# Second layer's experts: every quarter of the weights split into high and low halves, in five places, two low halves made by POOL

## What is computed

```python
router_probs = softmax(x @ gate_w + gate_b)
expert_values, expert_indices = top_k(router_probs, 2)
expert_values = expert_values / (sum(expert_values) + 1e-09)
h = gelu(x @ ew1[e] + eb1[e])            # 8 experts, 512 -> 2048
y = h @ ew2[e] + eb2[e]                  # 2048 -> 512
moe_out = sum over the two chosen experts of expert_values * y
```

## Time and profile before

| | |
|---|---|
| median of 3 runs | 2242.58 us (2241.16 to 2250.36) |
| profiled execution, its own time | 2245.86 us |
| its span, first to last instruction | 2244.1 us |
| PE busy | 2113.2 us (94%) |
| DVE busy | 1282.6 us (57%) |
| ACT busy | 1027.1 us (46%) |
| POOL busy | 519.6 us (23%) |
| the stage of the change | 1848.6 us to the end |

### The profile page before, as it was taken

The page is one execution under the profiler, slowest core; times in us unless marked ns, Lnnn a source line. Parts: engine busy times, 40 slices in busy tenths (PEclk is TensorE's granted clock), DMA queues, the critical chain, the costliest instruction groups (busy, mean ns, idle before and its releaser), DMA issues. The chain is left out here.

```text
span 2244.1 us, 39533 instructions
## 1 busy us (share of the span) xinstructions
PE 2113.2 (94%) x13342; PEld 1495.8 (67%) x13343; DVE 1282.6 (57%) x2751; ACT 1027.1 (46%) x2379; POOL 519.6 (23%) x503
## 2 busy tenths in 40 slices
PE   6999999997999999999888999999989889999998
PEld 4777777775954444444466777777769337777775
DVE  4677777776772222222347777777650127777776
ACT  2566666665321111111215666666653015666655
POOL 4000000001463554555420000000013002223331
PEclk9999999997999999999999999999989999999999
DMA  5011100012143999999821000000121426656661
GB/s 184 28 33 34 33 29 19 24 60 79 38 192 118 341 305 330 335 348 265 233 81 54 28 28 28 28 28 1 77 102 56 124 90 233 253 207 220 228 223 19
DMA packets 63756, 288.19 MB, mean 128 GB/s; under 512 B 10626, under 2 KB 10796, under 8 KB 44292
## 3 DMA queue, kind: packets, MB, share of 16 engines
q1 hardware_dynamic: 43892, 247.41, 29.9%
q0 software_dynamic: 19728, 38.97, 8.0%
HBM read 259.82 MB, written 32.93 MB: 130 GB/s over the span
## 5 line engine op out<-in xcount | busy, mean ns | idle before, releaser
L795 ACT ACTIVATE probs<-ps,less_max 100x360 f32<-100x360 f32 (+1 forms) x384 | 212.0, 561 | 166.9 <-DVE less_max L625 88.0
L1707 PE MATMUL pgu<-ring,xT 128*128 x560 | 266.0, 598 | 3.9 <-DVE xT L1787 2.0
L781 ACT ACTIVATE pTs<-pt 128x300 f32<-128x300 f32 x512 | 189.5, 425 | 125.6 <-PE pt L504 124.5
L1707 PEld LDWEIGHTS pgu<-ring,xT 128*128 128x128 f32 x560 | 100.2, 191 | 109.1 <-issue 108.7
L504 PE MATMUL pt<-ident,probs 100*128 100x100 f32 (+1 forms) x1152 | 137.6, 257 | 30.2 <-ACT pTs L781 26.7
L2094 DVE TENSOR_TENSOR ws_low<-first,ws_high 128x2048 fp32r<-128x2048 f32 x63 | 143.0, 2291 | 24.1 <-ACT ws_high L2025 24.1
L504 PEld LDWEIGHTS pt<-ident,probs 100*128 100x128 f32 (+1 forms) x1152 | 116.4, 141 | 60.4 <-issue 36.5
L381 PE MATMUL po<-first 128*128 128x512 f32 (+1 forms) x564 | 143.9, 404 | 1.4 <-DVEq L683 1.4
L381 PE MATMUL pp<-first 128*128 128x512 f32 x564 | 143.0, 402 | 1.2 <-DVE first L405 1.2
L625 DVE CUSTOM_DVE_ANT_0 ps<-ps,madd 100x362 f32<-100x362 f32 (+1 forms) x256 | 128.8, 565 | 22.9 <-PE ps L490 22.7
L377 PE MATMUL po<-first 128*128 128x362 f32 (+1 forms) x720 | 136.6, 339 | 2.8 <-DVE first L414 1.4
(11 more groups left out here) (330 smaller groups left out, 4208.9 us busy)
## 6 DMA issues: line engine op xcount, KB each, us to landing
ring<-in_l_ew SPq DMA_DIRECT2D x64, 1536.0 KB
first<-in_l_ew SPq DMA_DIRECT2D x32, 1024.0 KB, 8.5
w<-in_l_ew SPq DMA_DIRECT2D x32, 1024.0 KB, 8.7
xnT<-in_ctxT SPq DMA_DIRECT2D x14, 1444.0 KB, 6.8
first<-in_l_up SPq DMA_DIRECT2D x2, 4096.0 KB, 13.8
b<-in_l_eb SPq DMA_DIRECT2D x8, 1024.0 KB, 4.6
wd<-in_l_down SPq DMA_DIRECT2D x2, 2048.0 KB, 7.8
xn_rows<-mid SPq DMA_DIRECT2D x16, 200.0 KB
```

Source lines behind the costliest of these rows:

```text
L781: act.activation(pTs[:, g % 2, j, 3 * half:3 * half + 3, :].rearrange("k c q -> k (c q)"), pt[:, half, 0:3 * S], ACT.Copy).then_inc(t_out, 1)
L795: act.activation(probs[g % 2 * HPC + j][:, k0:k1], ps[j][0:S, 0:k1 - k0], ACT.Exp, bias=less_max[:, g, seg, j:j + 1], scale=-1.0 if masked ...
L1707: last = pe.matmul(pgu[p][:, :], xT[p][:, c, :], wgu[c], start=c == 0, stop=c == DC - 1)
```

## The change

All eight quarters are split now. The places are five: up quarters 0 to 3 in places 0, 1, 2, 3 and down quarters 0 to 3 in 0, 1, 2, 4. The two new places and `hb` lie at addresses that earlier stages use for other tiles (hence ACT's wait for `sum_begun`). The low halves of up quarter 3 and of down quarter 3 are made by POOL (`last_lows`), in its loop behind the gather and the scatter; DVE makes the other six. The plain FP32 products, `hT` and their semaphores go; PE no longer reads the tile's expert. On PE `down(0)` comes ahead of `turned(1)`. On ACT and DVE the order of the turns is new: DVE makes the low halves of the next tile's up quarters 0 and 1 ahead of yb and y, and that of quarter 2 behind them. The diff, cut to its core:

```diff
@@ -1841,20 +1841,22 @@
         xT = [sb(f"xT{part}", [P, DC, P], F32R) for part in ("_high", "_low")]
 
 
-        WS, WS_DOWN = (0, 1, 2, 1), {1: 0, 2: 2}
+
+
+        WS, WS_DOWN = (0, 1, 2, 3), (0, 1, 2, 4)
         ws = [[sb(f"ws{n}{part}", [P, 4, 512], F32R) for part in ("_high", "_low")] for n in range(2)]
...
         ws.append([sb(f"ws2{part}", [P, 4, 512], F32R) for part in ("_high", "_low")])
+        ws += env.more_ws
         x_high = sem("x_high")
         w_high, w_low = [sem(f"w_high{q}") for q in range(NQ)], [sem(f"w_low{q}") for q in range(NQ)]
-        hb = [sb(f"hb{n}", [P, 512]) for n in range(2)]
+        hb = env.hb
         h = [sb(f"h{n}", [P, 512]) for n in range(2)]
-        hT = sb("hT", [P, 2, FQ, P])
-        hs = [sb(f"hs{part}", [P, 2, FQ, P], F32R) for part in ("_high", "_low")]
+        hs = [sb(f"hs{part}", [P, NQ, FQ, P], F32R) for part in ("_high", "_low")]
         yb = sb("yb", [P, D])
-        d_high, d_low = ({q: sem(f"{name}{q}") for q in WS_DOWN} for name in ("d_high", "d_low"))
+        d_high, d_low = ([sem(f"{name}{q}") for q in range(NQ)] for name in ("d_high", "d_low"))
         hs_high, hs_ready = sem("hs_high"), sem("hs_ready")
         px = pb("px", [P, DC, P])
         pu = [pb(f"pu{n}", [P, 512]) for n in range(2)]
...
@@ -1894,10 +1896,8 @@
 
                         if q < NQ:
                             used, value = w_low[q], e and ended + 1
-                        elif q - NQ in WS_DOWN:
+                        else:
                             used, value = d_low[q - NQ], e and ended + 1
-                        else:
-                            used, value = down_mm, e and ended * NQ + (q - NQ + 1)
                         if q == NQ:
                             load(b1[:, :], b_up[e:e + 1, :].broadcast_to([P, I1]), b1_in, biased, e and ended * NQ + 1)
                         if e > 0 or q >= NQ:
@@ -1936,16 +1936,31 @@
                     pool.wait_ge(x_mm, t)
                     pool.sem_inc(passed, 1)
                     fetch(t)
+                def last_lows(t):
+
+                    pool.wait_ge(w_high[3], t + 1)
+                    pool.sem_inc(passed, 1)
+                    pool.tensor_tensor(ws[WS[3]][1][:, :, :], w[3][:, :, :], ws[WS[3]][0][:, :, :].bitcast(F32),
+                                       ALU.subtract).then_inc(w_low[3], 1)
+                    pool.wait_ge(d_high[3], t + 1)
+                    pool.sem_inc(passed, 1)
+                    pool.tensor_tensor(ws[WS_DOWN[3]][1][:, :, :], w[NQ + 3][:, :, :],
+                                       ws[WS_DOWN[3]][0][:, :, :].bitcast(F32), ALU.subtract).then_inc(d_low[3], 1)
 
                 pool.sem_inc(index_ready, 1)
+                pool.sem_inc(w_low[3], 1)
+                pool.sem_inc(d_low[3], 1)
                 fetch_next(1)
+                last_lows(0)
                 pool.wait_ge(env.sum_begun, 16 * G)
                 pool.sem_inc(passed, 1)
                 fetch_next(2)
                 add_rows(0, True)
+                last_lows(1)
                 with pool.Fori(3, n_tiles + 1) as t:
                     fetch_next(t)
                     add_rows(t - 2)
+                    last_lows(t - 1)
...
@@ -1963,8 +1978,6 @@
 
                 rows_turned(0)
                 with pe.Fori(0, n_tiles) as t:
-                    e = expert_of(pe, t)
-
                     def up(q):
                         pe.wait_ge(w_low[q], t + 2)
                         if q >= 2:
@@ -1979,7 +1992,7 @@
                     def turned(q):
                         pe.wait_ge(h_ready, t * NQ + q + 1)
                         if q >= 2:
-                            pe.wait_ge((hT_ready, hs_ready)[q % 2], t * 2 + 1)
+                            pe.wait_ge(hs_ready, t * NQ + q - 1)
                         for f in range(FQ):
                             last = pe.transpose(ph[q % 2][:, f, :], h[q % 2][:, f * P:(f + 1) * P], ident[:, :])
                         last.then_inc(h_mm, 1)
@@ -1987,14 +2000,9 @@
                     def down(q):
                         if q == 0:
                             pe.wait_ge(y_ready, t + 1)
-                        if q in WS_DOWN:
-                            pe.wait_ge(d_low[q], t + 2)
-                            pe.wait_ge(hs_ready, t * 2 + q // 2 + 1)
-                            parts = [(hs[i][:, q // 2], ws[WS_DOWN[q]][j]) for i, j in PARTS]
-                        else:
-                            pe.wait_ge(w_in[NQ + q], e * 16 + 16)
-                            pe.wait_ge(hT_ready, t * 2 + q // 2 + 1)
-                            parts = [(hT[:, q // 2], w[NQ + q])]
+                        pe.wait_ge(d_low[q], t + 2)
+                        pe.wait_ge(hs_ready, t * NQ + q + 1)
+                        parts = [(hs[i][:, q], ws[WS_DOWN[q]][j]) for i, j in PARTS]
                         for f in range(FQ):
                             for n, (hidden, weight) in enumerate(parts):
                                 last = pe.matmul(pd[:, :], hidden[:, f, :], weight[:, f, :], start=q + f + n == 0,
@@ -2005,8 +2013,8 @@
                     up(1)
                     turned(0)
                     up(2)
+                    down(0)
                     turned(1)
-                    down(0)
                     up(3)
                     turned(2)
                     down(1)
@@ -2054,27 +2062,31 @@
                     def hidden_out(q):
 
                         act.wait_ge(h_mm, t * NQ + q + 1)
-                        dst, ready = (hs[0], hs_high) if q in WS_DOWN else (hT, hT_ready)
-                        act.activation(dst[:, q // 2], ph[q % 2][:, :, :], ACT.Copy).then_inc(ready, 1)
+                        act.activation(hs[0][:, q], ph[q % 2][:, :, :], ACT.Copy).then_inc(hs_high, 1)
+                    split_high(t, 3, e)
+                    up_done(0)
+                    split_down_high(t, 0, e)
                     gelu(0)
+                    hidden_out(0)
                     up_done(1)
-                    split_high(t, 3, e)
+                    split_down_high(t, 1, e)
                     gelu(1)
-                    hidden_out(0)
-                    up_done(0)
-                    split_down_high(t, 1, e)
+                    up_done(2)
+                    split_down_high(t, 2, e)
                     gelu(2)
                     hidden_out(1)
-                    up_done(2)
-                    split_down_high(t, 2, e)
+
+                    act.wait_ge(down_mm, t * NQ + NQ)
+                    act.wait_ge(env.sum_begun, 16 * G)
+                    split_down_high(t, 3, e)
                     gelu(3)
                     hidden_out(2)
-                    up_done(3)
-                    split_high(t + 1, 1, e_next)
+                    down_done(0)
+                    split_high(t + 1, 0, e_next)
                     x_high_out(t + 1)
                     hidden_out(3)
                     down_done(1)
-                    split_high(t + 1, 0, e_next)
+                    split_high(t + 1, 1, e_next)
                     down_done(2)
                     split_high(t + 1, 2, e_next)
 
@@ -2084,9 +2096,8 @@
...
@@ -2117,26 +2128,27 @@
                         .then_inc(biased, 1)
 
                 def hidden_low(t, q):
-                    dve.wait_ge(hs_high, t * 2 + (q // 2 + 1))
-                    dve.tensor_tensor(hs[1][:, q // 2], ph[q % 2][:, :, :], hs[0][:, q // 2].bitcast(F32), ALU.subtract)\
+                    dve.wait_ge(hs_high, t * NQ + (q + 1))
+                    dve.tensor_tensor(hs[1][:, q], ph[q % 2][:, :, :], hs[0][:, q].bitcast(F32), ALU.subtract)\
                         .then_inc(hs_ready, 1)
 
                 def tile(t, very_first=False):
                     e = expert_of(dve, t)
                     dve.wait_ge(b1_in, e * 16 + 16)
                     add_bias(t, 0)
+                    split_down_low(t, 0)
+                    hidden_low(t, 0)
                     add_bias(t, 1)
-                    split_low(t, 3)
+                    split_down_low(t, 1)
                     add_bias(t, 2)
-                    split_down_low(t, 1)
+                    split_down_low(t, 2)
                     hidden_low(t, 1)
                     add_bias(t, 3)
-                    split_down_low(t, 2)
                     hidden_low(t, 2)
+                    x_low_out(t + 1)
+                    hidden_low(t, 3)
+                    split_low(t + 1, 0)
                     split_low(t + 1, 1)
-                    x_low_out(t + 1)
-                    split_low(t + 1, 0)
-                    split_low(t + 1, 2)
                     dve.wait_ge(b2_in, e * 16 + 16)
                     dve.wait_ge(down_mm, t * NQ + 2 * NQ)
                     dve.tensor_tensor(yb[:, :], pd[:, :], b2[:, :], ALU.add).then_inc(y_biased, 1)
@@ -2145,6 +2157,7 @@
                         dve.wait_ge(added, t * 16)
                     at = slice(t, t + 1) if isinstance(t, int) else bass.ds(t, 1)
```

(14 more changed lines are left out.)

## The result

| | before | after |
|---|---|---|
| median | 2243.3 us (2241.16 to 2250.36, 4 runs) | 2320.19 us (2315.19 to 2322.58, 4 runs) |
| profiled execution: time, span, mean granted clock | 2245.86, 2244.1, 0.976 | 2315.19, 2313.4, 0.961 |
| starts of xT_low apart in a steady tile | 25.54 us | 30.3 to 31.0 us, mean 30.65 (from the third on; the first two are 26.38 and 30.08) |

The change makes the kernel slower: ratio 1.0334, 95% interval 1.0304 to 1.0364. That is 77 us more, where 18 were forecast. The profiled spans are 69.3 us apart, and these come from three places. The fifteen spacings of xT_low have grown by 70.4, the end behind the last xT_low by 1.7 (1.9 forecast), and the first xT_low came 2.7 earlier. The profiled execution of after is the fastest of its four, 5 us under their median; the one of before lay above its own.

The account below looks back on a forecast made before the run. PE alone was taken to bound the experts' stage before; afterwards a DVE loop of 26.7 us a tile. First tile +0.7, thirteen tiles at +1.15 (+15), end +1.9: +17.6 on 2242.6 gives 2260 us, range 2238 to 2283.

Parts of the forecast that it names:

- PE's own sum: PE's products in one steady tile of the experts' stage: 24.1 us if PE never waits, 1.4 less than before.
- Work added elsewhere: Busy time per tile: ACT 19.3 us, DVE 20.3, both under 24; POOL two more subtractions of 4.6 us each.
- That the two exclude each other for whole instructions: POOL and DVE hold each other up on SBUF when DVE's instruction has two SBUF inputs or is the scaling y<-yb.
- Where the exclusion falls: POOL's up(3) subtraction runs behind DVE's low half of down(0) and holds that of down(1): 3.4 us without progress.
- The loop: DVE's turns from xT_low to hs_low(1), 22.4 us, plus 4.2 back to the next xT_low: 26.7 us a tile.
- The second subtraction at no cost: POOL's subtraction for down(3) runs from 17.7 to 22.3 us, before DVE's next low half at 23.0; costs nothing.
- First tile and end: First tile of the experts' stage 27.2 us against 26.56, +0.7; the last tile's end +1.9.
- Edits at nothing: The five places, ACT's new waits, SP's requests for down quarters and y_ready add no wait in the tiles.
- The first rival: POOL's subtraction goes ahead of down(0)'s low half; DVE loses up to 4.6 us, loop 27.9, 2277; chance 0.14 with the clock.
- the hold and the clock: POOL's worse exclusion of DVE, 2277, or a clock falling behind PE's new waits, 2280; chance 0.14 together.

Follow-up runs that it names:

- e6_no_subtraction: Changed kernel with POOL's subtractions left out in all tiles but the first two, older low halves used for up(3) and down(3); 2234.55 us.
- e1: Changed kernel with one wait more: POOL subtracts for up(3) only once DVE has made the low half of down(0); 2279.14 us.
- e9: Changed kernel with a one-column copy on POOL, and a wait for it, between the scatter and the subtraction for up(3); 2276.86 us.
- e4: Changed kernel, but DVE makes the low half of up(3) too, behind hb 1, and POOL only that of down(3); 2248.41 us.
- e2: Changed kernel with twelve products that nobody uses on PE between up(2) and down(0); 2293.53 us.
- e5: Changed kernel with POOL's subtraction for up(3) in two pieces of 1024 columns and a wait for the first piece between them; 2268.51 us.
- e3: Changed kernel with POOL's subtraction for up(3) as two instructions of 1024 columns, one straight behind the other; 2320.85 us.

## Why the prediction was wrong

**The direction was right, the size was not**: 2260 forecast, 18 us more than before, range 2238 to 2283, and 2320 measured, 77 us more. The prediction's steps one by one:

- **PE's own sum** (24.1): held, 24.20 in e6_no_subtraction.
- **Work added elsewhere**: held. DVE 20.14 (20.3 forecast) and ACT 19.69 (19.3) in the window of e6; POOL's subtraction of 2048 columns 4.61 (4.6), the line through the rows at 512 and 1024. The Trainium skill's 4497 ns (GPSIMD Engine Reference, "Elementwise — side-by-side cycle accounting") lies 0.1 us under it.
- **That the two exclude each other for whole instructions**: held. DVE loses 5.25 us in after and 3.3 in e1, the copy of e9 stands for 2.17.
- **Where the exclusion falls**: this step failed. Its clock times were good: the scatter was asked 2.9 us behind the start of up(0) (3.1 forecast) and ended at 5.6 (5.9), and DVE came to the low half of down(0) at 4.9 (5.0). What was wrong is the sentence that the subtraction, ready at 5.9, "finds DVE in the low half of down(0)". I took it that whoever is first by its start in the rows has the way to SBUF, and that POOL would ask for it when its scatter had ended. But POOL's instruction had been ready all along behind the scatter, and it was POOL that went first: the low half of down(0) took 7.53 us, PE waited 4.3 us ahead of down(0) and not 1.9 ahead of down(1), and the clock fell. e1 and e9 make the order that I had assumed, and the assumed loop comes out: 26.84 and 26.9 a tile against 26.7, with 1.57 us ahead of down(1).
- **The loop**: right in its arithmetic (e1), and not the one that ran.
- **The second subtraction at no cost**: held. It is 4.61 long beside no low half, and in e4, where only it is left, no low half of DVE's is lengthened.
- **First tile and end**: held. +0.7 and +1.9 forecast; from the first up(0) to the second it is 27.31 us against 26.56 in before, as forecast, and the end +1.7.
- **Edits at nothing**: held. No wait of PE's for a weight in the stage after its start, and ACT's new waits don't appear.

**The rival that came true** is the first one, and its price was wrong as well, in two ways. I gave it a loop of 27.9; by e2 the hold alone is 28.8. About two thirds of the difference is that I let DVE lose up to 4.6 us, the subtraction's length, although it is also held while the scatter runs out: 5.25. And I priced the hold and the clock as two ways to look alike, 2277 and 2280, when the one makes the other. A hold that lets PE stand for 4.3 us brings the clock down as well: 3.3 and 1.9 us a tile, 5.1 together, in fourteen tiles about the 70 us by which the spacings have grown. My argument against the clock's fall was a single wait of 2.59 us without one, and a PE busy for nine tenths; it is busy for 86% in after, and e1, e5 and e9 show waits of one length now with a fall and now without.

The first rival needed only 0.9 us by my own working, with the margin named as small, and it got a chance of 0.14 together with the clock. The argument against it, that the gather was held "in just this place", is about a POOL instruction that starts when DVE is already at work. In after DVE started when a POOL instruction was running and another was ready behind it. The earlier trace rows doesn't show that case: it has POOL's instructions each behind a wait of their own (0.64, 1.48 and 0.27 us of idle time). The trace of before has it once, in the first layer, and there DVE goes first. POOL and DVE:

```profile
632.66 2.37 POOL L1145 TENSOR_TENSOR after_xnT<-after_xnT,weight_high 128x928 fp32r<-128x928 f32 x1 [0.20 <-POOL after_xnT L1139]
634.99 2.91 POOL L1139 TENSOR_TENSOR after<-after,weight_low 128x928 fp32r<-128x928 f32 x1
...
633.36 2.95 DVE L1455 TENSOR_TENSOR mid<-tile_n,ends 1x1216 f32<-1x1216 f32 x1
```

DVE's instruction, 1.41 us when alone, ends 1.3 us behind POOL's first, and POOL's second, which no idle time parts from the first, is the one that is held (2.91 us, where the same size takes 1.74 at 644.72). So being ready behind another instruction doesn't always put POOL first, and a reading of this row would have spoken for my order.

The Trainium skill says of this (SBUF — State Buffer, "Who interferes with whom"): "Issue order, not op shape, decides who blocks." The runs agree as far as the same subtraction blocks DVE in after, and its second half is itself held in e5; they show besides that the order in which the rows start is not that order.

**What stays open.** Why the subtraction behind the scatter comes ahead of a DVE instruction whose row starts 0.2 us earlier, and the copy in e9 and the multiplication in the first layer behind one. The scatter alone does not hold DVE (e4), so it isn't simply that POOL had the way already. The subtraction may have begun to ask for its operands under the scatter's row, and the copy not; that is argued, and no run here shows it. Nor is it settled why the clock falls behind one wait of 1.57 us and not behind the next.

## What to carry to other kernels

Where two engines share a way to memory, a sum of busy times doesn't say who waits: write down, for every place where both want it, which of the two is *ready* first, and count an instruction that is queued behind another of its engine as one that may go first. If the margin is under a microsecond, take the worse order as the forecast, or put a wait into the kernel that fixes the order (e1 and e9: about 40 us each). And when an engine of matrix products gets a new wait, price the wait and the clock behind it as one sum.

## What the runs showed of the hardware that I had not expected

- **Subtractions that stand ready on POOL one behind the other can keep DVE out for all of them** (7.65 us in e3, with two pieces), and 0.18 us of waiting on POOL between them lets DVE in (5.34 in e5). The copy of e9, as ready behind the scatter, did not keep it out, nor did POOL's second multiplication at 634.99 in before.
- **An indirect DMA is held by DVE's two-input subtraction, but doesn't hold one**: 2.75 us for the scatter against 1.58, and 2.29 for the low half under it (e4).
- **Behind each pause of 4.2 to 4.4 us the clock fell to half, at once or within five products** (14 of 14 in after and in e3), **behind shorter ones only sometimes**: 2 of 14 at 2.0 to 2.1 us (e5), 4 of 15 (e1_gate) and 3 of 15 (e9_gap) at about 1.6 us, none of 14 at 1.5 to 1.6 us behind extra products (e2), none of 15 at 1.0 to 1.1 us (e4). A fall behind 1.57 us cost 1.6 us. Twelve useless products in the pause are worth 23 to 27 us (e2_busy against after).
